# Turned maxima and sums moved from the score ring into packed maximum units, copied by VectorE

## The chip, the cores and the metric

The kernel runs on one core of one Trainium2 chip. The metric is the device time of one execution in microseconds (us), as the median of several runs. A measurement of this kernel tells a change of about 0.2% from none.

## The reference

Two residual blocks run one after the other: differential attention and a gated feed-forward block, each followed by a layer norm.

```
x1  = layernorm(x + attn(x))        # x: 2 batches x 1024 tokens x 128
out = layernorm(x1 + ffn(x1))

# attn: 32 query/key heads of 4 dims, 16 value heads of 8 dims, causal
probs = softmax(q @ k.T * 4 ** -0.5 + causal mask)
attn  = (probs[head, 0] - lam * probs[head, 1]) @ v
attn  = rms_norm(attn) * rms_w * (1 - LAMBDA_INIT), then @ Wo

# ffn: xr, xk mix each token with the one before it
out = sigmoid(xr @ W_r.T) * (relu(xk @ W_k.T) ** 2 @ W_v.T)
```

## The kernel before

**Pairs and bursts.** The 64 (batch, head) score matrices are worked on two at a time, in 32 pairs (`NPAIR`). A pair n has 9 bursts (`NQ`), b = 0 to 8. `pair` of each engine writes the order out by hand: there is one stream of instructions on each engine, and semaphores between them. In burst b TensorE does four things, in this order:

1. `max_unit`: one of the 9 units (`NU`) that compute the scores from which the row maxima come. It runs ahead: in burst b stands unit b + 6 of the next pair for b below 3, and unit b - 3 of pair n + 2 from b = 3 on. The units alternate between two buffers `mx` of two PSUM banks each; unit m waits until VectorE has reduced unit m - 2 (`maxed`).
2. `score_burst`: the two score tiles of burst b (128 keys x 512 queries, one of each matrix), into the ring `ex` of 3 PSUM banks.
3. in burst 6 (`MAXIMA_AT`) `turn_maxima`, in burst 7 (`TURN_AT`) `turn_sums`, both described below.
4. `sum_burst`: the exponentials of four bursts ago times the values, summed in `acc`.

**Engines.** ScalarE takes the exponential of each score tile from `ex` to `e_buf` (L1075); in burst 3 it also copies the sums of the pair before out of `acc` (`take_sums`, L1002), between the two exponentials of that burst, once the sums of burst 3 are made. VectorE reduces each maximum unit to row maxima (L1191 for the plain units, 1024 elements per partition; L1179 for the diagonal ones, 768), combines them after the first unit of burst 3 (`combine`) and splits them in two bf16 parts after the next (`split_low`). GpSimd masks diagonals and normalises. SyncE's queue moves rows.

**Diagonal units.** Two of the nine units hold the diagonal blocks, packed by `diagonal_unit` into 384 of a bank's 512 columns: 8 matmuls of 64 columns (L641), 8 of half the partitions (L650), and 8 that add a mask (L660). They read the array's lower half of rows (partitions 64 to 127), like all maximum units; `score_burst` reads the upper half (0 to 63). Transposes (`turn_...`) use all 128. Before, the diagonal units are units 0 and 1, in bursts 3 and 4.

**What is turned.** `turn_maxima(n + 1)` transposes the combined row maxima (bf16, 128x128) in burst 6; the result is copied to `max_rows` and placed by DMA as rows of `qe`, which pair n + 1's first scores need (`place_maxima`). `turn_sums` transposes the sums of pair n - 1 in burst 7 (two f32 128x128); the result is copied to `o_tok`, from which GpSimd normalises.

**The ring before.** Score tile s of the ring may be written once the exponential of the tile three places before is done (`place_free`). The turned maxima and the turned sums take a place each between the tiles (and one place is skipped), so that a pair has 21 places; their place comes free by a ScalarE copy (`copy_maxima` L947, `store_sums` L1008).

```
def ex_slot(b, i):
    return 2 * b + i + 2 * (b > TURN_AT) + (b > MAXIMA_AT)
```

Of the kernel before, what the change touches and what calls it, by code (L numbers as in the profile page):

```python
# [106 lines left out]
def ex_slot(b, i):  # L107


    return 2 * b + i + 2 * (b > TURN_AT) + (b > MAXIMA_AT)  # L110


SUMS_SLOT = ex_slot(TURN_AT, 1) + 1
MAXIMA_SLOT = ex_slot(MAXIMA_AT, 1) + 1
RING = ex_slot(NQ - 1, 1) + 1
assert RING % EX_BANKS == 0
TILE_AT = {ex_slot(b, i): 2 * b + i for b in range(NQ) for i in range(2)}
# [9 lines left out]
def build(nc, x, Wq, Wk, Wv, Wo, lq1, lk1, lq2, lk2, rms_w, W_r, W_k, W_v, mu_r, mu_k, out):  # L127
# [24 lines left out]
    with ExitStack() as ctx:  # L152
# [84 lines left out]
        last_acc = wide[3][:, 0:HALF]  # L237

# [105 lines left out]
        def _(sp):  # L344
# [268 lines left out]
        def _(pe):  # L613
            def max_unit(g, pr, m):
# [49 lines left out]
            def place_free(n, at):  # L664

                at -= EX_BANKS
                while True:
                    if at < 0:
                        if isinstance(n, int) and n == 0:
                            return  # L670
                        at, n = at + RING, n - 1
                    if at in TILE_AT:
                        wait(pe, s["exped"], 2 * NQ * n + TILE_AT[at] + 1)
                        return
                    if at == SUMS_SLOT and not (isinstance(n, int) and n == 0):
                        wait(pe, s["o_stored"], n)
                        return
                    if at == MAXIMA_SLOT and not (isinstance(n, int) and n == NPAIR - 1):
                        wait(pe, s["max_copied"], n + 2)
                        return  # L680
                    at -= EX_BANKS

            def turn_maxima(n, bank):
# [109 lines left out]
            for u in range(NU + EARLY):  # L793
# [6 lines left out]
                if u == NU + 2:  # L800
                    turn_maxima(0, 2)
# [74 lines left out]
            def pair(g, par, pr):  # L876
# [4 lines left out]
                for b in range(NQ):  # L881
# [37 lines left out]
            turn_sums(NPAIR + 1, 0, last_acc)  # L919
# [18 lines left out]
        def _(act):  # L938
# [3 lines left out]

            def copy_maxima(n, bank):

                wait(act, s["max_rows_in"], 32 * n)
                act.wait_ge(s["max_turned"], n + 1)
                nc.scalar.copy(max_rows[:], ex[:, bank, :].bitcast(BF16)[0:2 * PAIR * NB, 0:P])\  # L947
                    .then_inc(s["max_copied"], 1)
# [47 lines left out]
            copy_maxima(0, 2)  # L996
# [7 lines left out]
            def store_sums(g, par, pr, turned):  # L1004

                act.wait_ge(s["acc_turned"], 2 * g + pr + 1)
                wait(act, s["norm_steps"], NORM_STEPS * (g - 1))
                nc.scalar.copy(o_tok[par][:, 16 * pr:16 * (pr + 1), :],  # L1008
                               turned.rearrange("p (a w) -> p a w", w=VPAD)[:, :, 0:VW + 1])\
                    .then_inc(s["o_stored"], 1)  # L1010
# [50 lines left out]
            def pair(g, par, pr):  # L1061
                static = isinstance(g, int)
                n = 2 * g + pr
                for b in range(NQ):
# [12 lines left out]
                    if b == MAXIMA_AT and not (static and n + 1 >= NPAIR):  # L1077
                        copy_maxima(n + 1, MAXIMA_SLOT % EX_BANKS)
# [341 lines left out]
```

## Time and profile before

| | us |
|---|---|
| median of 3 runs | 438.89 (438.17 to 438.91) |
| the profiled execution, own time | 438.0 |
| its span in the profile | 436.3 |
| TensorE / VectorE / ScalarE / GpSimd busy | 401.9 / 385.8 / 349.2 / 236.5 |

The span is what the trace covers; the execution's own time is 1.7 us longer. Busy time of TensorE is modelled from pipelined matmuls, so a high share does not say that it is at its peak. Three engines are busy over 80% of the span, so the question is which of them waits for which, and where in a pair.

### The profile page before, as it was taken

The numbers are of one execution on the slowest core, as the hardware profiler recorded it, in microseconds if no ns is written. First come the engines' busy times: TensorE is split into PE (matmuls) and PEld (weight loads), VectorE is DVE, ScalarE is ACT, GpSimd is POOL, SyncE is SP. The second block draws the span as 40 slices with busy tenths as digits, with TensorE's granted clock in tenths as the row PEclk, the third lists the DMA queues.
The fourth block names the chain that finished last, engine by engine and source line by source line (L and its number), as shares of the span: only waits on it lengthen the run. The fifth ranks groups of instructions, "written<-read, shape, count | busy, mean of one in ns | idle before, by whom it ended". The sixth has DMA issues, their size and how long they took to land.

```text
span 436.3 us, 17664 instructions
## 1 busy us (share of the span) xinstructions
PE 401.9 (92%) x6209; PEld 197.5 (45%) x6209; DVE 385.8 (88%) x551; ACT 349.2 (80%) x731; POOL 236.5 (54%) x574
## 2 busy tenths in 40 slices
PE   5856999999999999999999999999999999998882
PEld 3522444444444444444444444444444444444462
DVE  1889899999999999999999999999999999893485
ACT  3531799989999999999999999999999999885444
POOL 7200232566666666666666656666666665669422
PEclk9965599999999999999999999999999999998897
DMA  5565264321121111111111111111111121100002
GB/s 142 181 216 159 76 198 147 100 53 51 53 52 49 49 49 49 49 49 49 49 49 49 49 49 49 49 49 49 49 49 49 49 52 27 28 2 2 1 26 73
DMA packets 38800, 28.60 MB, mean 66 GB/s; under 512 B 22368, under 2 KB 27360, under 8 KB 38640
## 3 DMA queue, kind: packets, MB, share of 16 engines
q1 hardware_dynamic: 38176, 27.72, 22.8%
q10 hardware_dynamic: 592, 0.46, 0.4%
q8 instruction: 20, 0.33, 0.3%
q14 instruction: 12, 0.10, 0.1%
HBM read 20.39 MB, written 9.47 MB: 68 GB/s over the span
## 4 chain that ended last, share of the span: by engine, by line
PE 68%; ACT 14%; DVE 6%; issue 5%; DMA 2%; POOL 2%; SPq 1%; ACTq 0%; DVEq 0%; POOLq 0%
PE acc L732 31%; ACT e_buf L1075 13%; PE ex L702 11%; PE mx L629 10%; DVE part_max L1191 3%; PE mx L660 3%; PE ex L740 3%; PE mx L641 2%; PE mx L650 2%; PE ex L686 2%; SPq L335 1%; PE mx L866 1%; DMA x_tok<-in_L_attn_x 1%; PE mx L732 1%; DVE part_max L1179 1%
## 5 line engine op out<-in xcount | busy, mean ns | idle before, releaser
L1075 ACT ACTIVATE e_buf<-ex 128x512 f32<-128x512 f32 x576 | 304.1, 601 | 40.8 <-PE ex L702 40.1
L1191 DVE TENSOR_REDUCE part_max<-mx 128x2 f32<-128x1024 f32 (+2 forms) x224 | 263.9, 1220 | 12.4 <-PE mx L629 9.5
L553 POOL TENSOR_SCALAR_AFFINE_SELECT e_buf<-e_buf 128x256 f32<-128x256 f32 x256 | 100.2, 410 | 157.3 <-ACT e_buf L1075 157.3
L732 PE MATMUL acc<-e_buf,v_grp 128*32 128x256 f32 x2756 | 182.1, 353 | 1.2 <-POOL e_buf L553 1.2
L702 PE MATMUL ex<-qe,ke 26*128 26x512 bf16 (+3 forms) x768 | 148.1, 336 | 0.5 <-ACT e_buf L1075 0.2
L629 PE MATMUL mx<-km,qm 26*128 26x512 bf16 (+2 forms) x768 | 90.8, 301 | 6.2 <-DVE part_max L1191 4.5
L732 PEld LDWEIGHTS acc<-e_buf,v_grp 128*32 128x32 f32 x2756 | 64.9, 109 | 49.4 <-issue 40.7
L1179 DVE TENSOR_REDUCE part_max<-mx 128x12 f32<-128x768 f32 x64 | 61.1, 954 | 7.0 <-PE mx L660 6.1
L629 PEld LDWEIGHTS mx<-km,qm 26*128 26x128 bf16 x768 | 26.8, 93 | 86.5 <-issue 64.0
L702 PEld LDWEIGHTS ex<-qe,ke 26*128 26x128 bf16 x768 | 46.7, 91 | 20.3 <-ACT e_buf L1075 8.6
L536 POOL TENSOR_TENSOR r_rms<-sq_eps,minus_half 128x16 f32<-128x16 f32 x15 | 43.7, 2910 | 0.0
L660 PE MATMUL mx<-mask,pick 32*128 32x192 bf16 (+1 forms) x512 | 26.1, 222 | 0.0
L641 PE MATMUL mx<-km,qm 29*128 29x64 bf16 x512 | 18.9, 193 | 2.9 <-DMA km<-k_rows 2.0
L641 PEld LDWEIGHTS mx<-km,qm 29*128 29x128 bf16 x512 | 11.3, 94 | 21.7 <-issue 11.8
L660 PEld LDWEIGHTS mx<-mask,pick 32*128 32x128 bf16 x512 | 18.4, 95 | 2.8
L650 PE MATMUL mx<-km,qm 29*64 29x64 bf16 x512 | 16.9, 204 | 0.0
L583 POOL TENSOR_TENSOR rs<-ve,minus_half 128x4 f32<-128x4 f32 x8 | 8.5, 1056 | 14.3 <-DVE ve L1268 14.2
L541 POOL TENSOR_TENSOR attn_n<-attn,r_rms 128x32 f32 (+1 forms) x60 | 12.8, 245 | 3.7 <-POOL r_rms L536 3.7
L740 PE MATMUL ex<-identf,o_rows 128*128 128x128 f32 x62 | 13.6, 300 | 0.0
L686 PE MATMUL ex<-identb,turn_max 128*128 128x128 bf16 x32 | 7.4, 231 | 5.6 <-ACT e_buf L1075 4.3
L947 ACT COPY max_rows<-ex 32x128 bf16<-32x128 bf16 x32 | 7.8, 243 | 5.8 <-PE ex L686 5.8
L1002 ACT COPY o_rows<-acc 128x256 f32<-128x256 f32 x31 | 11.6, 373 | 0.9
(144 smaller groups left out, 297.9 us busy)
## 6 DMA issues: line engine op xcount, KB each, us to landing
qm<-q_rows SPq DMA_DIRECT2D x32, 128.0 KB, 2.5
km<-k_rows SPq DMA_DIRECT2D x32, 128.0 KB, 2.7
qe<-q_rows SPq DMA_DIRECT2D x32, 128.0 KB, 2.5
ke<-k_rows SPq DMA_DIRECT2D x32, 128.0 KB, 2.6
q_rows<-part_q SPq DMA_DIRECT2D x6, 256.0 KB, 2.7
k_rows<-part_k SPq DMA_DIRECT2D x6, 256.0 KB, 2.8
q_rows<-part_q SPq DMA_DIRECT2D x6, 192.0 KB
k_rows<-part_k SPq DMA_DIRECT2D x6, 192.0 KB
```

The costliest lines, as they stand in the source:

```text
L536: pool.tensor_tensor(r_rms[:], sq_eps[:], minus_half[:], ALU.pow).then_inc(s["norm_steps"], 1)
L553: pool.affine_select(out=e, in_=e, compare_op=ALU.is_ge, fill=0.0, base=0, pattern=[[0, PAIR], [1, P]], channel_multiplier=-1)\
L629: last = pe.matmul(bank[:, jj, col:col + P * nk], qm[pr][rows, P * qb:P * (qb + 1)], km[pr][rows, P * kb:P * (kb + nk)], start=i == 0, sto ...
L641: pe.matmul(bank[:, jj, BLOCK * r:BLOCK * (r + 1)], qm[pr][rows, t:t + P], km[pr][rows, t:t + BLOCK], start=r == 0, stop=False, skip_group ...
L650: pe.matmul(bank[own, jj, col:col + BLOCK], qm[pr][rows, t:t + BLOCK], km[pr][rows, t:t + BLOCK], start=False, stop=False, skip_group_chec ...
L660: last = pe.matmul(out[:, :, own], pick[rows, c, :], cols, start=False, stop=c == 3, skip_group_check=True)
L702: scored = pe.matmul(ex[:, ex_slot(b, i) % EX_BANKS, col:col + w], ke[pr][rows, P * kb:P * (kb + 1)], qe[pr][rows, q1 - w:q1], start=col = ...
L732: last = pe.matmul(out, v, e, start=first, stop=over, skip_group_check=True)
L740: last = pe.transpose(turned[:, P * i:P * (i + 1)], o_rows[pr][:, P * i:P * (i + 1)], identf[:])
L1075: nc.scalar.activation(e_buf[:, b, i, :], ex[:, ex_slot(b, i) % EX_BANKS, :], ACT.Exp).then_inc(s["exped"], 1)
L1179: nc.vector.tensor_reduce(part_max[pr][:, :, matmuls, 0, :], scores[:, :, 0:BLOCK * ENTRIES] .rearrange("p s (a b) -> p s a b", b=BLOCK), ...
L1191: nc.vector.tensor_reduce(place, scores, AX.X, ALU.max).then_inc(s["maxed"], 1)
```

## The change

The nine maximum units are put in another order: the two diagonal ones become units 3 and 4, so that they stand in bursts 6 and 7 (and three plain units in bursts 3 to 5). The turned maxima are written into the free columns 384 to 511 of unit 3's first bank, the turned sums into those of both banks of unit 4; each transpose is issued at the end of its unit, ahead of the burst's scores, and the unit's semaphore goes up with it. VectorE copies both out, right before it reduces the unit. The ring keeps its 18 score tiles alone. On SyncE's queue `place_maxima` moves ahead of `move_high`, which now waits for unit 4's reduce. For the last pairs, which have no maximum units behind them, the turned data go to other free banks, and VectorE's copies stand between its steps of the first norms.

```diff
 MAX_UNITS = [
-    (0, None),
-    (1, None),
     ([(0, 4, 0, 4)], (slice(1, 2), 1, slice(0, 1))),
     ([(0, 5, 0, 4)], (slice(1, 2), 1, slice(1, 2))),
     ([(0, 6, 0, 4)], (slice(1, 2), 1, slice(2, 3))),
+    (0, None),
+    (1, None),
     ([(0, 7, 0, 4)], (slice(1, 2), 1, slice(3, 4))),
     ([(0, 2, 0, 2), (256, 6, 4, 2)], (slice(0, 2), 2, slice(2, 3))),
     ([(0, 3, 0, 2), (256, 7, 4, 2)], (slice(0, 2), 2, slice(3, 4))),
...
-    return 2 * b + i + 2 * (b > TURN_AT) + (b > MAXIMA_AT)
-
-
-SUMS_SLOT = ex_slot(TURN_AT, 1) + 1
-MAXIMA_SLOT = ex_slot(MAXIMA_AT, 1) + 1
+    return 2 * b + i
+
+
 RING = ex_slot(NQ - 1, 1) + 1
 assert RING % EX_BANKS == 0
-TILE_AT = {ex_slot(b, i): 2 * b + i for b in range(NQ) for i in range(2)}
+
+
+
+MAXIMA_UNIT, SUMS_UNIT = (at + EARLY - NU for at in (MAXIMA_AT, TURN_AT))
+SIDE = BLOCK * ENTRIES
+assert all(isinstance(MAX_UNITS[m][0], int) for m in (MAXIMA_UNIT, SUMS_UNIT)) and MAXIMA_UNIT < SUMS_UNIT
...
+        last_maxima = wide[3].bitcast(BF16)
+        late_sums = wide[2][:, 0:HALF]
+
+        def halves_of(t):
+            return [t[:, P * i:P * (i + 1)] for i in range(2)]
...
-            wait(sp, s["maxed"], NU * n + 2)
+            wait(sp, s["maxed"], NU * n + SUMS_UNIT + 1)
...
+                if not isinstance(n, int) or n + 1 < NPAIR:
+                    place_maxima(sp, n + 1, 1 - pr, g + pr)
                 if not isinstance(n, int) or n + 2 < NPAIR:
                     move_high(sp, n + 2, pr)
-                if not isinstance(n, int) or n + 1 < NPAIR:
-                    place_maxima(sp, n + 1, 1 - pr, g + pr)
...
                     last = diagonal_unit(pr, bank, matmuls)
+                    if m == MAXIMA_UNIT and not (isinstance(n, int) and n < 1):
+                        last = turn_maxima(n - 1, bank[:, 0, :].bitcast(BF16)[:, 2 * SIDE:2 * SIDE + P])
+                    if m == SUMS_UNIT and not (isinstance(n, int) and n < 3):
+                        last = turn_sums(n - 2, 1 - pr, [bank[:, i, SIDE:BANK] for i in range(2)])
...
             def place_free(n, at):
...
+                if isinstance(n, int) and 2 * NQ * n + at < EX_BANKS:
+                    return
+                wait(pe, s["exped"], 2 * NQ * n + at - EX_BANKS + 1)
+
+            def turn_maxima(n, turned):
 
                 pe.wait_ge(s["max_split"], n + 1)
-                pe.transpose(ex[:, bank, :].bitcast(BF16)[:, 0:P],
-                             turn_max[:].rearrange("p e r -> p (e r)"), identb[:]).then_inc(s["max_turned"], 1)
+                return pe.transpose(turned, turn_max[:].rearrange("p e r -> p (e r)"), identb[:])
 
             def score_burst(g, pr, b):
 
...
                     score_burst(g, pr, b)
-                    if b == MAXIMA_AT and not (static and n + 1 >= NPAIR):
-                        place_free(n, MAXIMA_SLOT)
-                        turn_maxima(n + 1, MAXIMA_SLOT % EX_BANKS)
-                    if b == TURN_AT and not (static and n == 0):
-                        place_free(n, SUMS_SLOT)
-                        turn_sums(n, 1 - pr, ex[:, SUMS_SLOT % EX_BANKS, 0:HALF])
+                    if b == MAXIMA_AT and static and n == NPAIR - 2:
+                        pe.wait_ge(s["maxed"], NU * NPAIR)
+                        turn_maxima(NPAIR - 1, last_maxima[:, 0:P]).then_inc(s["max_turned"], 1)
+                    if b == TURN_AT and static and n >= NPAIR - 2:
+                        if n == NPAIR - 1:
+                            pe.wait_ge(s["r_gated"], 1)
+                            pe.wait_ge(s["o_stored"], NPAIR - 2)
+                        turn_sums(n, 1 - pr, halves_of(late_sums)).then_inc(s["acc_turned"], 1)
                     if b == HALF_AT and static and n == NPAIR - 1:
-                        turn_sums(NPAIR, pr, acc[:, 0:HALF])
...
             def take_sums(n, pr):
 
                 act.wait_ge(s["summed"], NQ * (n + 1))
-                wait(act, s["acc_turned"], n - 1)
+                wait(act, s["o_stored"], n - 1)
...
-                    if b == MAXIMA_AT and not (static and n + 1 >= NPAIR):
-                        copy_maxima(n + 1, MAXIMA_SLOT % EX_BANKS)
-                    if b == TURN_AT and not (static and n == 0):
-                        store_sums(g - 1 + pr, par if pr == 1 else 1 - par, 1 - pr,
-                                   ex[:, SUMS_SLOT % EX_BANKS, 0:HALF])
...
-                wait(dve, s["max_turned"], n)
                 nc.vector.tensor_reduce(turn_max[:, 0].rearrange("p (a e) -> p a e", e=4), blocks, AX.X, ALU.max)\
                     .then_inc(s["combined"], 1)
+
+            def copy_maxima(n, turned):
+
+                wait(dve, s["max_rows_in"], 32 * n)
+                nc.vector.tensor_copy(max_rows[:], turned[0:2 * PAIR * NB]).then_inc(s["max_copied"], 1)
+
+            def store_sums(g, par, pr, turned):
+
+                wait(dve, s["norm_steps"], NORM_STEPS * (g - 1))
+                nc.vector.tensor_copy(o_tok[par][:, 16 * pr:16 * (pr + 1), :].rearrange("p (s a) w -> p s a w", s=2),
+                                      turned.rearrange("p s (a w) -> p s a w", w=VPAD)[:, :, :, 0:VW + 1])\
+                    .then_inc(s["o_stored"], 1)
+
+            def take_maxima(n, pr):
+
+                dve.wait_ge(s["max_scored"], NU * (n + 1) + MAXIMA_UNIT + 1)
+                bank = mx_of(n + 1, 1 - pr, MAXIMA_UNIT)
+                copy_maxima(n, bank[:, 0, :].bitcast(BF16)[:, 2 * SIDE:2 * SIDE + P])
+
+            def take_turned(g, par, pr):
+
+                dve.wait_ge(s["max_scored"], NU * (2 * g + pr + 3) + SUMS_UNIT + 1)
+                store_sums(g, par, pr, mx_of(2 * g + pr + 3, 1 - pr, SUMS_UNIT)[:, :, SIDE:BANK])
...
+                    if m - NU == MAXIMA_UNIT:
+                        take_maxima(n + 1, 1 - pr)
+                    if m - NU == SUMS_UNIT and not (static and n == 0):
+                        take_turned(g - 1 + pr, par if pr == 1 else 1 - par, 1 - pr)
...
             norm_attn(0)
+            dve.wait_ge(s["max_turned"], 1)
+            copy_maxima(NPAIR - 1, last_maxima[:, 0:P])
             norm_attn(1)
+            dve.wait_ge(s["acc_turned"], 1)
+            store_sums(NG - 2, 0, 1, late_sums.rearrange("p (s t) -> p s t", s=2))
             apply1(0)
...
             norm_ffn(0)
+            dve.wait_ge(s["acc_turned"], 2)
+            store_sums(NG - 1, 1, 0, late_sums.rearrange("p (s t) -> p s t", s=2))
             normalise_half(0)
```

**TensorE, bursts 6 and 7 of pair 1.** Before (mx is the maximum unit, ex the score tiles, acc the sums):

```order
L629 MATMUL mx<-km,qm 128x512 x2
L702 MATMUL ex<-qe,ke 128x512 x2
L686 MATMUL ex<-identb,turn_max 128x128
L732 MATMUL acc<-e_buf,v_grp 32x128 x8
L629 MATMUL mx<-km,qm 128x512 x2
L702 MATMUL ex<-qe,ke 128x512 x2
L740 MATMUL ex<-identf,o_rows 128x128 x2
L732 MATMUL acc<-e_buf,v_grp 32x256 x4
```

After, up to the transposes of burst 7 (behind them follow the scores and the sums, as in burst 6):

```order
L652 MATMUL mx<-km,qm 128x64 x8
L661 MATMUL mx<-km,qm 64x64 x8
L671 MATMUL mx<-mask,pick 128x6x32 x4
L671 MATMUL mx<-mask,pick 128x2x32 x4
L684 MATMUL mx<-identb,turn_max 128x128
L699 MATMUL ex<-qe,ke 128x512 x2
L729 MATMUL acc<-e_buf,v_grp 32x128 x8
L652 MATMUL mx<-km,qm 128x64 x8
L661 MATMUL mx<-km,qm 64x64 x8
L671 MATMUL mx<-mask,pick 128x6x32 x4
L671 MATMUL mx<-mask,pick 128x2x32 x4
L736 MATMUL mx<-identf,o_rows 128x128 x2
```

The transposes moved from between scores and sums to between the unit and the scores, and the units of these bursts changed from 2 plain matmuls to 24 small ones.

**VectorE, one pair.** Before, from the third unit of a pair (4 + 2 + 1 plain units) to the next pair's two diagonal ones and `split_low`:

```order
L1191 TENSOR_REDUCE part_max<-mx 128x2 x4
L1191 TENSOR_REDUCE part_max<-mx 128x4 x2
L1191 TENSOR_REDUCE part_max<-mx 128x4x2
L1179 TENSOR_REDUCE part_max<-mx 128x2x6
L1198 TENSOR_REDUCE row_max<-part_max 128x16
L1201 TENSOR_REDUCE turn_max<-part_max 128x16
L1179 TENSOR_REDUCE part_max<-mx 128x2x6
L1207 TENSOR_TENSOR turn_max<-row_max,turn_max 128x16
```

After, from the third unit (burst 5) to the ninth, and the next pair's first:

```order
L1165 TENSOR_REDUCE part_max<-mx 128x2
L1180 COPY max_rows<-mx 32x128
L1153 TENSOR_REDUCE part_max<-mx 128x2x6
L1185 COPY o_tok<-mx 128x144
L1153 TENSOR_REDUCE part_max<-mx 128x2x6
L1165 TENSOR_REDUCE part_max<-mx 128x2
L1165 TENSOR_REDUCE part_max<-mx 128x4 x2
L1165 TENSOR_REDUCE part_max<-mx 128x4x2
L1165 TENSOR_REDUCE part_max<-mx 128x2
```

Two copies out of `mx` were added, each ahead of the reduce of a diagonal unit.

**VectorE at the end of the program, behind the last split.** Before, the norms of the first two chunks (`norm_attn(0)`, `norm_attn(1)`) and then `apply1` (L1275):

```order
L1288 TENSOR_TENSOR xT<-mx,x_tok 128x512
L1258 BN_STATS st<-xT 128x6 x4
L1263 BN_AGGR mv<-st 128x2 x4
L1268 TENSOR_SCALAR ve<-mv 128x4
L1288 TENSOR_TENSOR xT<-mx,x_tok 128x512
L1258 BN_STATS st<-xT 128x6 x4
L1263 BN_AGGR mv<-st 128x2 x4
L1268 TENSOR_SCALAR ve<-mv 128x4
L1275 TENSOR_SCALAR x<-xT,mv,rs 128x128 x8
```

After:

```order
L1290 TENSOR_TENSOR xT<-mx,x_tok 128x512
L1260 BN_STATS st<-xT 128x6 x4
L1265 BN_AGGR mv<-st 128x2 x4
L1270 TENSOR_SCALAR ve<-mv 128x4
L1180 COPY max_rows<-mx 32x128
L1290 TENSOR_TENSOR xT<-mx,x_tok 128x512
L1260 BN_STATS st<-xT 128x6 x4
L1265 BN_AGGR mv<-st 128x2 x4
L1270 TENSOR_SCALAR ve<-mv 128x4
L1185 COPY o_tok<-mx 128x144
L1277 TENSOR_SCALAR x<-xT,mv,rs 128x128 x8
```

The copy of the last pair's maxima stands between the two norms, and a copy of turned sums ahead of `apply1`.

## Rows read from the trace of the kernel before

**Rows 1.** Windows: stretch, length; busy us (instructions) by engine; clock, DMA share, GB/s.

```profile
74.58:372.11 297.53, 292.95 (x5052) 138.83 (x5049) 283.36 (x325) 270.51 (x568) 182.89 (x462) 1.00 0.20 50
```

**Rows 2.** Timeline of ScalarE: start, busy us, instructions; maxima copies of pairs 1, 30.

```profile
51.95 0.24 ACT L947 COPY max_rows<-ex 32x128 bf16<-32x128 bf16 x1
...
372.11 0.24 ACT L947 COPY max_rows<-ex 32x128 bf16<-32x128 bf16 x1
```

**Rows 3.** Timeline of TensorE (weight loads apart), one pair, bursts 3 to 8.

```profile
201.51 0.29 PE L641 MATMUL mx<-km,qm 29*128 29x64 bf16 x8
...
201.95 0.39 PE L702 MATMUL ex<-qe,ke 26*128 26x512 bf16 x2
202.02 0.30 PE L660 MATMUL mx<-mask,pick 32*128 32x192 bf16 x6
202.27 0.64 PE L732 MATMUL acc<-e_buf,v_grp 128*32 128x128 f32 x12
202.84 0.29 PE L641 MATMUL mx<-km,qm 29*128 29x64 bf16 x8
...
205.37 0.39 PE L629 MATMUL mx<-km,qm 26*128 26x512 bf16 x2
...
206.02 0.23 PE L686 MATMUL ex<-identb,turn_max 128*128 128x128 bf16 x1 [0.18 <-ACT e_buf L1075]
206.18 0.64 PE L732 MATMUL acc<-e_buf,v_grp 128*32 128x128 f32 x16
206.76 0.39 PE L629 MATMUL mx<-km,qm 26*128 26x512 bf16 x2
...
207.29 0.44 PE L740 MATMUL ex<-identf,o_rows 128*128 128x128 f32 x2
207.65 0.64 PE L732 MATMUL acc<-e_buf,v_grp 128*32 128x256 f32 x8
208.23 0.39 PE L629 MATMUL mx<-km,qm 26*128 26x512 bf16 x2
...
212.58 0.29 PE L641 MATMUL mx<-km,qm 29*128 29x64 bf16 x8
```

**Rows 4.** Timeline of ScalarE, the same pair.

```profile
203.06 0.37 ACT L1002 COPY o_rows<-acc 128x256 f32<-128x256 f32 x1
203.33 3.58 ACT L1075 ACTIVATE e_buf<-ex 128x512 f32<-128x512 f32 x7
206.80 0.24 ACT L947 COPY max_rows<-ex 32x128 bf16<-32x128 bf16 x1
207.22 1.08 ACT L1075 ACTIVATE e_buf<-ex 128x512 f32<-128x512 f32 x2 [0.18 <-PE ex L702]
```

**Rows 5.** Timeline of VectorE, the same pair.

```profile
198.81 3.49 DVE L1191 TENSOR_REDUCE part_max<-mx 128x4 f32<-128x1024 f32 x3
202.46 0.96 DVE L1179 TENSOR_REDUCE part_max<-mx 128x12 f32<-128x768 f32 x1 [0.16 <-PE mx L660]
203.33 0.29 DVE L1198 TENSOR_REDUCE row_max<-part_max 128x16 f32<-128x80 f32 x1
...
203.74 0.95 DVE L1179 TENSOR_REDUCE part_max<-mx 128x12 f32<-128x768 f32 x1
...
204.68 3.73 DVE L1191 TENSOR_REDUCE part_max<-mx 128x2 f32<-128x1024 f32 x3
```

**Rows 6.** The page's part 5: the reduces of plain units.

```profile
L1191 DVE TENSOR_REDUCE part_max<-mx 128x2 f32<-128x1024 f32 (+2 forms) x224 | 263.9, 1220 | 12.4 <-PE mx L629 9.5
```

**Rows 7.** Timeline of VectorE near the end, pair 30.

```profile
383.26 0.68 DVE L1288 TENSOR_TENSOR xT<-mx,x_tok 128x512 f32<-128x512 f32 x1
...
385.37 2.44 DVE L1275 TENSOR_SCALAR x<-xT,mv,rs 128x128 f32<-128x128 f32 x8
```

**Rows 8.** Timeline of TensorE, the same stretch.

```profile
384.57 0.23 PE L686 MATMUL ex<-identb,turn_max 128*128 128x128 bf16 x1
...
386.80 0.66 PE L831 MATMUL mx<-identf,x 128*128 128x128 f32 x4
```

More of the change, by code:

```diff
@@ L377, in _ @@
             load_max_rows(sp, 2, 0)
+            place_maxima(sp, 0, 0, 0)
             move_high(sp, 1, 1)
-            place_maxima(sp, 0, 0, 0)
             fill_rows(1, s["rows_b1"])
@@ L664, in place_free @@
             def place_free(n, at):
[L666 to L683, printed above, removed]
+                if isinstance(n, int) and 2 * NQ * n + at < EX_BANKS:
+                    return
+                wait(pe, s["exped"], 2 * NQ * n + at - EX_BANKS + 1)
+            def turn_maxima(n, turned):
                 pe.wait_ge(s["max_split"], n + 1)
-                pe.transpose(ex[:, bank, :].bitcast(BF16)[:, 0:P],
-                             turn_max[:].rearrange("p e r -> p (e r)"), identb[:]).then_inc(s["max_turned"], 1)
+                return pe.transpose(turned, turn_max[:].rearrange("p e r -> p (e r)"), identb[:])
             def score_burst(g, pr, b):
@@ L739, in turn_sums @@
                 for i in range(2):
-                    last = pe.transpose(turned[:, P * i:P * (i + 1)], o_rows[pr][:, P * i:P * (i + 1)], identf[:])
-                last.then_inc(s["acc_turned"], 1)
+                    last = pe.transpose(turned[i], o_rows[pr][:, P * i:P * (i + 1)], identf[:])
+                return last
             def turn_x(ch):
@@ L799, in _ @@
                     turn_weights()
-                if u == NU + 2:
-                    turn_maxima(0, 2)
             pe.wait_ge(s["wt_scaled"], 1)
@@ L887, in pair @@
                     score_burst(g, pr, b)
-                    if b == MAXIMA_AT and not (static and n + 1 >= NPAIR):
-                        place_free(n, MAXIMA_SLOT)
-                        turn_maxima(n + 1, MAXIMA_SLOT % EX_BANKS)
-                    if b == TURN_AT and not (static and n == 0):
-                        place_free(n, SUMS_SLOT)
-                        turn_sums(n, 1 - pr, ex[:, SUMS_SLOT % EX_BANKS, 0:HALF])
+                    if b == MAXIMA_AT and static and n == NPAIR - 2:
[6 more added lines that the diff above has]
+                        turn_sums(n, 1 - pr, halves_of(late_sums)).then_inc(s["acc_turned"], 1)
                     if b == HALF_AT and static and n == NPAIR - 1:
-                        turn_sums(NPAIR, pr, acc[:, 0:HALF])
+                        turn_sums(NPAIR, pr, halves_of(acc[:, 0:HALF])).then_inc(s["acc_turned"], 1)
                     if b >= LAG:
@@ L918, in _ @@
             sum_burst(NG - 1, 1, 1, NQ - 1)
-            turn_sums(NPAIR + 1, 0, last_acc)
+            turn_sums(NPAIR + 1, 0, halves_of(last_acc)).then_inc(s["acc_turned"], 1)
             turn_attn(2)
@@ L941, in _ @@
             act.dma_start(wv_sb[:], Wv).then_inc(s["wv_in"], 16)
[L943 to L948, printed above, removed]
             def high(m):
@@ L995, in _ @@
             last.then_inc(s["wt_scaled"], 1)
-            copy_maxima(0, 2)
             def take_sums(n, pr):
                 act.wait_ge(s["summed"], NQ * (n + 1))
-                wait(act, s["acc_turned"], n - 1)
+                wait(act, s["o_stored"], n - 1)
                 nc.scalar.copy(o_rows[pr][:], acc[:, 0:HALF]).then_inc(s["acc_copied"], 1)
[L1004 to L1010, printed above, removed]
             def take_half(c):
                 act.wait_ge(s["summed"], NQ * (NPAIR - 1) + (FIRST_HALF if c == 0 else NQ))
-                act.wait_ge(s["acc_turned"], NPAIR - 1)
+                act.wait_ge(s["o_stored"], NPAIR - 2 + c)
                 nc.scalar.copy(o_rows[1 - c][:], acc[:, 0:HALF] if c == 0 else last_acc)\
@@ L1019, in store_half @@
             def store_half(c):
-                act.wait_ge(s["acc_turned"], NPAIR + c)
+                act.wait_ge(s["acc_turned"], 3 + c)
                 act.wait_ge(s["norm_steps"], NORM_STEPS * (NG - 2))
@@ L1219, in _ @@
             for u in range(NU + EARLY):
+                if u == NU + MAXIMA_UNIT:
+                    take_maxima(0, 0)
                 max_unit(0, u // NU, u % NU)
```

## Prediction

> **What bounds the kernel now.** I read the windows first, then the timelines of one steady pair, engine by engine, then the end of the program. Over 297.53 us of steady state TensorE is busy 292.95 us, VectorE 283.36, ScalarE 270.51, all at TensorE's full granted clock (1.00, its 2.4 GHz level) [rows 1]: no engine has much room, and the average does not say who waits. One pair takes (372.11 - 51.95) / 29 = 11.04 us [rows 2].
>
> TensorE's timeline shows two things. First, bursts that the ring holds up: in burst 6 the transpose of the maxima starts 0.65 us after the burst (205.37 to 206.02) and was released by an exponential; in burst 7 the transposes (207.29) stand behind ScalarE's copy of the maxima (206.80 + 0.24). Bursts 6 and 7 take 1.39 and 1.47 us [rows 3, 4]. Second, a burst with a diagonal unit takes 1.33 us (201.51 to 202.84), and in it the scores (201.95) start while the mask matmuls are still going (202.02 to 202.32): unit and scores lie side by side [rows 3].
>
> VectorE is not the bound. Its reduces follow each other at (3.49 - 1.22) / 2 = 1.14 us when nothing holds them [rows 5, 6]; a diagonal one takes 0.87 (202.46 to 203.33), the combining 0.41, the last diagonal reduce and the split 0.94. That is 7 x 1.14 + 0.87 + 0.41 + 0.94 = 10.20 us, so 0.84 of 11.04 is waiting for TensorE [rows 2, 5].
>
> **The change part by part.**
>
> *ScalarE's copies go.* The next work starts 0.42 us after the maxima copy (206.80 to 207.22) [rows 4], of which TensorE's lateness is a part. ScalarE has room already (270.51 of 297.53), so this pays only through the ring.
>
> *The ring.* No score waits for a copy any more. Free of all ring waits, a plain burst is scores to sums 0.32 (201.95 to 202.27), sums 0.58 (207.65 to 208.23): 0.90 us. So burst 6 could gain 1.39 - 0.90 - 0.16 = 0.33 and burst 7 1.47 - 0.90 - 0.37 = 0.20, if nothing else moved (0.16 and 0.37 are the transposes' own shares: 206.02 to 206.18 and 207.29 to 207.65) [rows 3].
>
> *VectorE's two copies.* The trace has no such copy on VectorE. A reduce of 1024 elements takes 1.22 us and one of 768 takes 0.96, so an element is 1.02 ns, and 128 or 144 elements would be 0.31 and 0.32 us alone, 0.23 and 0.24 in a row (0.08 of a reduce's 1.22 overlaps the next). From the other side, ScalarE's same copy takes 0.24 [rows 4 to 6]. I take 0.20 to 0.24 each; the floor of VectorE's pair is then 10.62 to 10.68 us, still below 11.04. They cost nothing while VectorE waits for TensorE ahead of the second diagonal reduce, which the next part makes longer; without that cover they cost 0.44 a pair.
>
> *The diagonal units meet the transposes.* This is the term that decides. The transposes need all array rows, so they wait for the masks, and the scores behind them wait for the transposes: the side by side of unit and scores is gone in both bursts. Masks end at 202.32, 0.81 after the burst's start; the next matmul of other rows starts 0.07 before a modelled end (202.34 against 202.27), so the transpose starts at 0.74. Scores follow 0.16 later (0.90), sums at 1.22, end at 1.22 + 0.57 = 1.79 for burst 6. Burst 7 has 0.37 for 0.16: 2.00 [rows 3]. Together 3.79 us, against 2.86 now. In return bursts 3 and 4 hold plain units, 0.90 each instead of 1.33, where nothing else holds them.
>
> A page speaks against this term. The Trainium skill, TensorE: Matmul & The Clock Gate, in its step-by-step part of what a matmul's phases are for, says that matmuls stay in program order and only weight loads are pulled ahead. The masks stand ahead of the scores in the program, and the trace has scores at 201.95 ahead of six masks at 202.02 [rows 3], so here I go by the rows. By the page there was no overlap to lose, and the two bursts would be 1.33 + 0.16 and 1.33 + 0.37; that is the first rival.
>
> *Does ScalarE give bursts 3 to 5 away?* Count from the start of burst 3. Burst 4 starts at 0.90. The copy of the sums starts 0.22 into it (202.84 to 203.06), 1.12; the next exponential 0.27 later (203.06 to 203.33), 1.39. With burst 3's first exponential at 0.46 (206.76 to 207.22) those of burst 4 start at 1.88 and 2.37 (3.58 us for 7, so 0.49 apart). The second score of burst 5 needs the bank of the one at 1.88: 1.88 + 0.60 + 0.06 = 2.54. Sums at 2.86, burst 6 at 3.43 [rows 3, 4]. So these three bursts cost 3.43, not 2.70: ScalarE's pace, not TensorE's. (0.60 is one exponential's duration by 1.08 for two at 0.49; 0.06 is the hand-over between engines, an estimate from TensorE to ScalarE: 206.76 + 0.39 to 207.22 is 0.07.)
>
> Bursts 8, 0, 1, 2 take 4.35 now (208.23 to 212.58) [rows 3]; I leave them so. TensorE's and ScalarE's loop is then 3.43 + 3.79 + 4.35 = 11.57 us.
>
> *VectorE's loop, counted apart.* From burst 8's start its unit is ready for VectorE at 0.43 (a plain unit takes 0.39, and a hand-over). Then reduces of units 5, 6, 7, 8, 0 (5 x 1.14), combining 0.41, unit 1 in full 1.22 and a hand-over 0.06: 7.82, when TensorE may write unit 3, that is start burst 6. With bursts 6 and 7: 7.82 + 3.79 = 11.61 [rows 3, 5, 6]. The two loops are equal within my reading; I take 11.59.
>
> *The end.* In pair 30 VectorE's `norm_attn(1)` starts at 383.26; now the copy of the maxima stands ahead of it and waits for TensorE's transpose, 384.57 + 0.23. With the copy, the norm starts near 385.04, 1.78 later, and the second copy adds 0.2. `apply1` starts at 385.37, and TensorE takes its result at 386.80 without room to speak of: 1.7 us on the path [rows 7, 8]. Queued behind the waiting copy are both applies and the token mixing, for which TensorE waits.
>
> *Queue of SyncE.* `place_maxima` no longer stands behind `move_high`; the maxima's copy falls 1.3 us into burst 6, before 1.67 (205.37 to 206.80 + 0.24), and the next pair's first scores are later: no wait. `move_high` now starts after burst 7, and its data are needed after the next unit 0, some 5 us on: nothing.
>
> **Sum.** Pairs 0 to 29 have the new bursts: 30 x (11.59 - 11.04) = 16.5, the end 1.7: 438.0 + 18.2 = 456.2 for the profiled execution. The median lies 0.9 above that execution, so 457.
>
> **Rivals.**
> 1. *No overlap to lose* (condition: bursts 6 and 7 at 1.49 and 1.70). TensorE's loop 3.43 + 3.19 + 4.35 = 10.97, VectorE's 7.82 + 3.19 = 11.01: -0.03 x 30 + 1.7, so 439.7 at the median. For it: the starts of matmuls may be modelled. Against: the burst of 1.33 with 24 small matmuls fits only if its scores cost it nothing. Chance 0.07, most of it no change.
> 2. *Only part is lost*: the transposes slip in behind the masks and the scores follow without the gaps of 0.1 at each change. Bursts of 1.6 and 1.8 give a pair of 11.2 to 11.3, and 445 to 449. Chance 0.18.
> 3. *Faster: the freed ring is what counts.* If the transposes hide beside masks and scores altogether, bursts 6 and 7 are 2.66, VectorE's loop 10.48, and the pair falls to VectorE's floor, 10.65: 438.9 - 11.7 + 1.7 = 429. It decides at 3.17 us for both bursts (7.82 + 3.17 + 0.06 of the end = 11.04); above, the kernel is slower. For it are 0.53 us of ring waits in these bursts; against it, the transposes need every row of the array. Chance 0.06.
> 4. *Both loops add up*: each held up by the other in turn, or VectorE's copies uncovered (0.44 a pair): 12.0, 469. Chance 0.07; the two loops pass through different waits, but both end at burst 6's start.
>
> **How the numbers follow.** Forecast (452 to 462) 0.62, rivals as given. A measurement of this kernel tells 0.2%, 0.9 us. Faster: rival 3 and a little of rival 1, 0.08; same: 0.05; slower: 0.87. The range 445 to 463 takes in rival 2 and leaves out the others.
>
> **What would show it.** In the profile after: maxima transposes 11.5 to 11.7 us apart; in bursts 6 and 7 scores starting 0.9 and 1.1 us after the burst's start, and bursts of 1.8 and 2.0; ScalarE idle there for 0.5 us and more each; bursts 3 to 5 held by waits for exponentials; VectorE waiting ahead of the second diagonal unit, the copies 0.2 us each; `norm_attn(1)` 1.8 us later. Scores that start beside the masks, or VectorE without waits, would make the prediction wrong.

## The result, and the profile after

The change makes the kernel slower: 459.92 us (median of 4 runs, 458.17 to 461.11) against 438.53 for the kernel before beside it (4 runs, 438.09 to 438.91), a ratio of 1.0485 (95% interval 1.0443 to 1.0527). The prediction was 457 us in a range of 445 to 463. Disturbed executions are left out of the ratios here and below: one of e7's at 587.69 us, and two of the kernel before beside e9, at 443.97 and 449.48.

The profiled execution took 458.17 us with a span of 456.4, 20.1 more than before. The windows of its trace, with the columns of [rows 1]:

```profile
53.00:59.50 6.50, 6.50 (x86) 2.16 (x82) 3.61 (x4) 4.00 (x8) 1.39 (x4) 0.50 0.13 26
76.96:390.67 313.71, 306.37 (x5056) 141.31 (x5050) 288.73 (x379) 259.07 (x513) 182.28 (x459) 0.99 0.19 49
104.00:114.10 10.10, 9.80 (x173) 4.71 (x165) 9.23 (x13) 8.29 (x17) 6.70 (x21) 1.00 0.21 55
114.10:117.50 3.40, 3.40 (x34) 0.82 (x36) 2.42 (x4) 2.19 (x5) 0.72 (x2) 0.50 0.09 5
```

The second row is the stretch from the 4th to the 31st maxima transpose: 313.71 us for 27 pairs, where 297.53 stood in [rows 1]. One pair takes 11.58 us, the median distance of two of these transposes; before it was 11.02, the mean 297.53 / 27 (the median there is 11.04). The other rows come up under the clock, below.

TensorE's timeline, one steady pair from burst 6 to the next burst 6, and then the last maxima transpose and the first transposes behind the first norm:

```profile
204.72 0.29 PE L652 MATMUL mx<-km,qm 29*128 29x64 bf16 x8 [0.16 <-DVE part_max L1165]
...
205.13 0.40 PE L671 MATMUL mx<-mask,pick 32*128 32x192 bf16 x8
205.46 0.23 PE L684 MATMUL mx<-identb,turn_max 128*128 128x128 bf16 x1
205.62 0.39 PE L699 MATMUL ex<-qe,ke 26*128 26x512 bf16 x2
...
206.51 0.29 PE L652 MATMUL mx<-km,qm 29*128 29x64 bf16 x8
...
207.25 0.44 PE L736 MATMUL mx<-identf,o_rows 128*128 128x128 f32 x2
207.62 0.39 PE L699 MATMUL ex<-qe,ke 26*128 26x512 bf16 x2
...
208.51 0.39 PE L640 MATMUL mx<-km,qm 26*128 26x512 bf16 x2
208.52 0.56 PE L699 MATMUL ex<-qe,ke 26*128 26x384 bf16 x4
...
212.63 0.39 PE L640 MATMUL mx<-km,qm 26*128 26x512 bf16 x2
...
216.30 0.29 PE L652 MATMUL mx<-km,qm 29*128 29x64 bf16 x8
...
404.52 0.23 PE L684 MATMUL mx<-identb,turn_max 128*128 128x128 bf16 x1
...
408.43 0.66 PE L825 MATMUL mx<-identf,x 128*128 128x128 f32 x4 [1.84 <-DVE x L1277]
```

Bursts 6 and 7 last 206.51 - 204.72 = 1.79 and 208.51 - 206.51 = 2.00 us. In both, scores (205.62, 207.62) start only behind the transpose (205.46, 207.25). In [rows 3] they started beside the masks. The scores of burst 8 (208.52) start with their unit (208.51). In the kernel before, whose burst 8 started at 208.23, they did not:

```profile
208.36 0.56 PE L702 MATMUL ex<-qe,ke 26*128 26x384 bf16 x4
```

There the first of them waited for the second exponential of burst 7, which ended at 207.22 + 1.08 = 208.30 [rows 4]: counted in places of the ring, that tile stood three before. In the changed kernel the tile three before is one of burst 6.

VectorE's timeline of the same stretches:

```profile
205.88 0.20 DVE L1180 COPY max_rows<-mx 32x128 bf16<-32x128 bf16 x1
206.01 0.94 DVE L1153 TENSOR_REDUCE part_max<-mx 128x12 f32<-128x768 f32 x1
207.82 0.31 DVE L1185 COPY o_tok<-mx 128x144 f32<-128x144 f32 x1 [0.88 <-PE mx L736]
208.04 0.95 DVE L1153 TENSOR_REDUCE part_max<-mx 128x12 f32<-128x768 f32 x1
208.94 5.75 DVE L1165 TENSOR_REDUCE part_max<-mx 128x2 f32<-128x1024 f32 x5
...
215.02 1.22 DVE L1165 TENSOR_REDUCE part_max<-mx 128x2 f32<-128x1024 f32 x1
...
404.79 0.21 DVE L1180 COPY max_rows<-mx 32x128 bf16<-32x128 bf16 x1 [1.31 <-PE mx L684]
404.93 0.67 DVE L1290 TENSOR_TENSOR xT<-mx,x_tok 128x512 f32<-128x512 f32 x1
...
407.04 0.31 DVE L1185 COPY o_tok<-mx 128x144 f32<-128x144 f32 x1
407.26 0.85 DVE L1277 TENSOR_SCALAR x<-xT,mv,rs 128x128 f32<-128x128 f32 x3
```

The copy of the sums waits 0.88 us for TensorE's transposes (207.82). Behind it runs a stretch in which VectorE waits for nothing: 5 plain reduces (208.94), the combining and one more reduce (215.02), and right behind that TensorE starts burst 6 (216.30); burst 6 of the pair shown waited 0.16 us for such a reduce (204.72). Near the end, the copy of the last maxima waits 1.31 us, and the second norm (404.93) behind it.

ScalarE's timeline of the pair:

```profile
206.04 1.08 ACT L1054 ACTIVATE e_buf<-ex 128x512 f32<-128x512 f32 x2 [1.02 <-PE ex L699]
208.04 5.65 ACT L1054 ACTIVATE e_buf<-ex 128x512 f32<-128x512 f32 x11 [0.92 <-PE ex L699]
```

It waits 1.02 and 0.92 us for the scores of bursts 6 and 7, where [rows 4] had 0.18.

### The profile page after: what moved, and what is told of

Same layout as the page of the kernel before. It is cut to its first block, busy times and chain, and to the rows that moved or that the text cites. A ratio compares the mean times of both kernels' runs of the same rounds, so it can differ in the third digit from the quotient of the medians.

```text
span 456.4 us, 17652 instructions
## 1 busy us (share of the span) xinstructions
PE 417.3 (91%) x6209; PEld 200.9 (44%) x6209; DVE 393.2 (86%) x614; ACT 335.8 (74%) x668; POOL 236.8 (52%) x574
## 4 chain that ended last, share of the span: by engine, by line
PE 45%; DVE 29%; issue 14%; SPq 3%; POOL 2%; DMA 2%; DVEq 1%; ACT 1%; ACTq 1%; POOLq 0%
DVE part_max L1165 20%; PE acc L729 14%; PE ex L699 7%; PE mx L671 5%; PE mx L640 4%; DVE part_max L1153 4%; PE mx L652 3%; PE mx L661 3%; PE mx L736 2%; SPq L342 2%; DVE row_max L1172 1%; PE mx L684 1%; DVE turn_max L1174 1%; PE mx L860 1%; DMA x_tok<-in_L_attn_x 1%
## 5 line engine op out<-in xcount | busy, mean ns | idle before, releaser
L1054 ACT ACTIVATE e_buf<-ex 128x512 f32<-128x512 f32 x576 | 299.9, 601 | 75.3 <-PE ex L699 75.0
L1185 DVE COPY o_tok<-mx 128x144 f32<-128x144 f32 x31 | 9.5, 307 | 25.4 <-PE mx L736 25.4
L736 PE MATMUL mx<-identf,o_rows 128*128 128x128 f32 x64 | 14.0, 300 | 0.5 <-ACT o_rows L995 0.5
L661 PEld LDWEIGHTS mx<-km,qm 29*64 29x64 bf16 x512 | 9.8, 106 | 3.5
```

The costliest lines, as they stand in the source:

```text
L661: pe.matmul(bank[own, jj, col:col + BLOCK], qm[pr][rows, t:t + BLOCK], km[pr][rows, t:t + BLOCK], start=False, stop=False, skip_group_chec ...
L736: last = pe.transpose(turned[i], o_rows[pr][:, P * i:P * (i + 1)], identf[:])
L1054: nc.scalar.activation(e_buf[:, b, i, :], ex[:, ex_slot(b, i) % EX_BANKS, :], ACT.Exp).then_inc(s["exped"], 1)
```

## The experiments

Each ran beside the kernel before, whose median was 437.18 us beside e1 to e4, 438.08 beside e5 to e8 and 437.84 beside e9. "A pair" is the median distance of two maxima transposes; the start is the time up to the 4th of them, the end that behind the 32nd. Pair, start and end come from one profiled execution each; the medians come from 4 to 12 executions.

**e1: the transposes behind the scores.** The change, with each transpose of bursts 6 and 7 issued between scores and sums, as before.

```diff
-                    max_unit(g + 1, pr, m - NU)
+                    max_unit(g + 1, pr, m - NU, later)
                     score_burst(g, pr, b)
+                    if later:
+                        turn_into(n + 2, pr, m - NU).then_inc(s["max_scored"], 1)
```

> The changed kernel with one thing moved: in bursts 6 and 7 of the steady pairs the transposes are issued behind the burst's scores, ahead of the sums; they still go into the free columns of the diagonal units, and VectorE still copies them. Lost overlap (my theory): the scores lie beside the masks again, bursts 6 and 7 fall from 1.79 and 2.00 us to 1.49 and 1.70, the pair from 11.58 to 11.0 (VectorE's loop 7.82 + 3.19), the median from 460 to 442 to 444. Rival, the place in the free columns or VectorE's copies cost the time: 458 to 461, no change. Rival, the order of the units costs it: also no change.

Measured: 445.59 us, ratio 1.0177 (1.0128 to 1.0226); a pair 11.25. TensorE's timeline:

```profile
209.54 0.29 PE L658 MATMUL mx<-km,qm 29*128 29x64 bf16 x8
...
209.98 0.39 PE L705 MATMUL ex<-qe,ke 26*128 26x512 bf16 x2
210.05 0.30 PE L677 MATMUL mx<-mask,pick 32*128 32x192 bf16 x6
210.30 0.23 PE L690 MATMUL mx<-identb,turn_max 128*128 128x128 bf16 x1
...
211.04 0.29 PE L658 MATMUL mx<-km,qm 29*128 29x64 bf16 x8
...
212.73 0.39 PE L646 MATMUL mx<-km,qm 26*128 26x512 bf16 x2
```

Scores (209.98) start beside the masks (210.05) again, and the bursts last 1.50 and 1.69: 0.60 less than 3.79, as expected. The pair gives back only 0.33 of it, so that the time lies above the 442 to 444 that were expected. VectorE's timeline, one pair earlier, says where the rest went:

```profile
201.12 0.31 DVE L1196 COPY o_tok<-mx 128x144 f32<-128x144 f32 x1 [0.62 <-PE mx L742]
...
202.21 5.74 DVE L1176 TENSOR_REDUCE part_max<-mx 128x2 f32<-128x1024 f32 x5
```

Burst 8 started at 201.49, so its unit was ready near 201.92. VectorE still copied sums and reduced the diagonal unit until 202.21: its stretch from there takes 8.05 us instead of 7.79. With shorter bursts the sums' copy, which stands between the transposes and that reduce, is on the path.

**e2: the order alone.** The kernel before with the new order of units and of SyncE's queue. Ring, transposes' places and ScalarE's copies are those of before.

```diff
 MAX_UNITS = [
-    (0, None),
-    (1, None),
     ([(0, 4, 0, 4)], (slice(1, 2), 1, slice(0, 1))),
     ([(0, 5, 0, 4)], (slice(1, 2), 1, slice(1, 2))),
     ([(0, 6, 0, 4)], (slice(1, 2), 1, slice(2, 3))),
+    (0, None),
+    (1, None),
```

> The kernel before with one part of the change alone: the new order of the nine units (diagonal ones in bursts 6 and 7) and the order of SyncE's queue that goes with it; the turned data still take places in the score ring, behind the scores, and ScalarE copies them. Lost overlap: it is kept here, so the pair stays near the one before, 11.0 to 11.3 us, 438 to 447 at the median. Rival, two heavy units ahead of two transposes are too much by themselves, wherever the transposes stand: 11.5 or more, 453 or more.

Measured: 446.4 us, ratio 1.0201 (1.0151 to 1.0251); a pair 11.24. TensorE starts bursts 6, 7 and 8 at 199.95, 201.44 and 203.22, and VectorE's timeline shows waits for the second diagonal unit and for the plain one behind it:

```profile
202.29 0.96 DVE L1179 TENSOR_REDUCE part_max<-mx 128x12 f32<-128x768 f32 x1 [0.17 <-PE mx L660]
203.66 5.92 DVE L1191 TENSOR_REDUCE part_max<-mx 128x2 f32<-128x1024 f32 x5 [0.41 <-PE mx L629]
```

Two heavy bursts side by side (1.49 and 1.78) leave VectorE short, and its stretch of 7.97 us then holds up the next burst 6 (211.19). So the order, with SyncE's queue, costs 0.22 a pair. The stretch is 0.18 longer than the 7.79 of the change. Here the ring still holds up burst 8: its scores start 0.25 behind the unit (203.22),

```profile
203.47 0.56 PE L702 MATMUL ex<-qe,ke 26*128 26x384 bf16 x4
```

the unit of the next burst follows at 204.53, 1.31 later where the change had 1.08, and VectorE, which could have gone on at 203.66 + 1.14 = 204.80, starts its second plain reduce at 204.96. e1 (no ring places, VectorE's copies) and e2 (the ring and the copies of before) have nearly the same pair: what the freed ring gives in that stretch, 0.18, the sums' copy takes again (8.05 in e1).

**e3: a lighter VectorE.** The change, with the reduces of the first two plain units reading half of each stretch of columns. This leaves out a part of the row maxima.

```diff
                     scores = scores[:].rearrange("p s (a b) -> p s a b", a=nh * ne)
+                    if m in (0, 1):
+                        scores = scores[:, :, :, 0:BANK // (2 * nh * ne)]
```

> The changed kernel with VectorE relieved: the reduces of the first two plain units of a pair read half of their columns (the other half of those maxima is left out), 1.07 us less of VectorE a pair. If VectorE's loop alone holds burst 6 back, TensorE starts it when the sums of burst 5 end, 0.2 to 0.3 us earlier: the pair takes 11.3 us, the median 451 to 453. If the loop over ScalarE's pace in bursts 3 to 5 is as long (11.57, as the prediction has it), nothing moves: 458 to 461.

Measured: 454.06 us, ratio 1.0361 (1.0302 to 1.042), a little above the 451 to 453 expected of the case in which VectorE's loop binds alone; pairs alternate between 11.35 and 11.43. The only row of TensorE's steady timeline that still waits is

```profile
211.55 0.64 PE L729 MATMUL acc<-e_buf,v_grp 128*32 128x256 f32 x8 [0.24 <-ACT o_rows L989]
```

That is the other loop, TensorE and ScalarE: 11.39 us, 0.19 under the pair of the change. So the steady pairs of the change are bound by VectorE's loop alone, and the two are not equal.

**e4: ScalarE's copies at the end.** The change, with the turned data of the last pairs copied by ScalarE instead of between VectorE's norms.

```diff
-            dve.wait_ge(s["max_turned"], 1)
-            copy_maxima(NPAIR - 1, last_maxima[:, 0:P])
             norm_attn(1)
```

> The changed kernel with its last part undone: for the last pairs ScalarE copies the turned maxima and sums, at the places where it did before, and VectorE's norms follow each other. If the copies between VectorE's norms cost 1.7 us, the median falls by 1.5 to 2, to 458; if the wait that they cause is hidden further down, no change.

Measured: 456.34 us, ratio 1.0435 (1.0379 to 1.0491), 0.5% under the change, with intervals that overlap. The end takes 48.78 us instead of 51.89. Not all of that is the copies' doing: the end of the change has a stretch of 3.4 us at 1.2 GHz (from 434.95 on), and that of e4 ran at a granted clock of 1.00 from 406.00 to 450.80. The second pair of norms is applied 30.33 us behind the last maxima transpose in the change and 28.82 in e4, so ahead of that stretch the copies cost 1.5 us; the difference grows to 3.1 only behind it.

**e5: the copies doubled.** The change, with each of VectorE's two copies made once more into a spare buffer.

```diff
+                nc.vector.tensor_copy(spare_max[:], turned[0:2 * PAIR * NB])
                 nc.vector.tensor_copy(max_rows[:], turned[0:2 * PAIR * NB]).then_inc(s["max_copied"], 1)
```

> The changed kernel with VectorE's two copies made twice each (the second time into buffers that nobody reads). My prediction held the copies hidden by VectorE's wait ahead of the second diagonal unit. In the trace after, the maxima's copy lies there, but the sums' copy stands behind that wait, and VectorE's next plain reduce starts at 208.94, when its diagonal reduce ends and when its unit is ready alike. If both are hidden: no change, 458 to 461. If the sums' copy is on VectorE's loop: 0.22 us a pair, 11.8 a pair, 464 to 468. If both are: 11.98 a pair, 470 to 473.

Measured: 464.84 us, ratio 1.0592 (1.0543 to 1.0641); a pair 11.75. VectorE's timeline:

```profile
208.68 0.21 DVE L1182 COPY spare_max<-mx 32x128 bf16<-32x128 bf16 x1
208.82 0.20 DVE L1183 COPY max_rows<-mx 32x128 bf16<-32x128 bf16 x1
...
210.68 0.31 DVE L1188 COPY spare_tok<-mx 128x144 f32<-128x144 f32 x1 [0.79 <-PE mx L738]
210.90 0.30 DVE L1190 COPY o_tok<-mx 128x144 f32<-128x144 f32 x1
```

Two more copies, 0.14 and 0.22 from start to start, make the pair 0.17 longer, by most of the second one. The maxima's copy is covered by the wait for the sums' transposes (0.79 where it was 0.88); the sums' copy is not.

**e6: the heavy units apart.** The change, with a plain unit in burst 7 and the second diagonal unit with the turned sums in burst 8.

```diff
     (0, None),
+    ([(0, 7, 0, 4)], (slice(1, 2), 1, slice(3, 4))),
     (1, None),
-    ([(0, 7, 0, 4)], (slice(1, 2), 1, slice(3, 4))),
```

> The changed kernel with the second diagonal unit, and the turned sums with it, moved one burst on, from burst 7 to burst 8, a plain unit between the two heavy ones; the transposes still stand ahead of the scores. If two heavy bursts in a row starve VectorE (it waits 0.88 us ahead of the second), the wait shrinks by 0.4 to 0.8 and the pair goes to about 11.2, 447 to 450. If only the sum of TensorE's work between the loop's ends counts, nothing moves much: 11.5 or more, 456 or more.

Measured: 457.15 us, ratio 1.0418 (1.0372 to 1.0463); a pair 11.52. TensorE starts bursts 6, 7, 8 and 0:

```profile
204.95 0.29 PE L652 MATMUL mx<-km,qm 29*128 29x64 bf16 x8
...
206.75 0.39 PE L640 MATMUL mx<-km,qm 26*128 26x512 bf16 x2
...
207.81 0.29 PE L652 MATMUL mx<-km,qm 29*128 29x64 bf16 x8
...
209.81 0.28 PE L640 MATMUL mx<-km,qm 26*128 26x256 bf16 x2
```

1.80, 1.06 and 2.00 us: the same work, in other places. Spreading alone is worth 0.06 a pair. The theory that VectorE starves behind two heavy bursts in a row does not explain the time of the change: the rival held, as long as the transposes stand ahead of the scores.

**e7: apart, and transposes last.** e6 with e1's place for the transposes; the diffs are theirs.

> The same spread with the transposes behind the scores, as in the first experiment. If starvation and lost overlap are both real and add, this has neither: the pair near 11.0, the median 438 to 441, the same as the kernel before. If spreading brings nothing, 445 as with the transposes moved alone.

Measured: 441.59 us, ratio 1.0073 (1.0046 to 1.01), a little above the 438 to 441 that were expected; a pair 11.02, that of the kernel before. What is left over lies in the start (76.52 us, before 73.67) and the end. TensorE starts bursts 6, 7, 8 and 0, and the scores beside the masks (208.28):

```profile
207.85 0.29 PE L658 MATMUL mx<-km,qm 29*128 29x64 bf16 x8
...
208.28 0.39 PE L705 MATMUL ex<-qe,ke 26*128 26x512 bf16 x2
...
209.34 0.39 PE L646 MATMUL mx<-km,qm 26*128 26x512 bf16 x2
...
210.24 0.29 PE L658 MATMUL mx<-km,qm 29*128 29x64 bf16 x8
...
211.94 0.28 PE L646 MATMUL mx<-km,qm 26*128 26x256 bf16 x2
```

and VectorE has a wait of 0.30 left (0.40 one pair earlier), so its floor is near 10.7:

```profile
211.48 0.31 DVE L1196 COPY o_tok<-mx 128x144 f32<-128x144 f32 x1 [0.30 <-PE mx L742]
```

Moving the transposes is worth 0.50 a pair here and 0.33 in e1.

**e8: e7 with ScalarE's copies at the end** (e4's edit).

> The same, with ScalarE's copies for the last pairs. 1.5 to 3 us less than without: 436 to 439. With the freed ring this is the version that could pass the kernel before; if the ring is worth as little as the trace of the first two experiments says, it does not by more than 1 us.

Measured: 438.18 us, ratio 0.9989 (0.9966 to 1.0012): no change from before that can be told. The end takes 49.50 us, 2.8 less than e7's 52.29. Here too the clock has a part: e7's end has a stretch of 6.8 us at 1.2 GHz (391.9 to 398.7), in which TensorE is busy throughout, and e8's one of 3.4 (from 415.2). The two were not run at like clocks, so the copies' own share of the 2.8 is not shown.

**e9: the first maxima turned early.** e8, with the first pair's maxima turned right behind their split and copied by ScalarE, as before the change.

```diff
                     turn_weights()
+                if u == NU + 2:
+                    turn_maxima(0, ex[:, 2, :].bitcast(BF16)[:, 0:P]).then_inc(s["max_turned"], 1)
```

> Of the profiled execution's 20.1 us over the kernel before, 3.3 fell ahead of the fourth pair, and e7 and e8, whose steady pairs are as fast as before, still lose 2.6 to 2.9 there. Theory: that is the first turned maxima, which wait for a diagonal unit of the next pair (turned at 39.8 instead of 38.1, first scores at 42.9 instead of 41.9 in e8). This kernel is e8 with the first pair's maxima turned by themselves, right behind their split, into a free bank, and copied by ScalarE, as before the change: turned at 38.6, first scores at 41.8, the start 1.0 to 1.4 us shorter than e8's (76.3 to 75.1), the kernel at 436.0 to 437.5, ratio 0.994 to 0.998. Rival: the lost start is the order of the units alone (three plain units ahead of the diagonal ones, so that the combining comes 0.4 to 0.6 us later and TensorE's wait ahead of the first pairs is given by SyncE's and GpSimd's work): no gain over e8, ratio 0.998 to 1.001.

Measured: 438.63 us, ratio 1.0003 (0.9977 to 1.0029): no gain over e8, as the rival had it. The start takes 77.86 us, not less than e8's 76.27. The transpose stands 0.22 us behind the split now (39.81 to 40.03; in e8 38.56 to 39.82), but the split itself was 1.25 later in this execution, and the first scores (43.84) came 3.81 behind the transpose instead of 3.12. In this execution the clock had also fallen to its 1.2 GHz level earlier, at 24.4 instead of 26.1. With 12 and 10 executions at the same median within 0.1%, one transpose is not what the start loses; that it is the order of the units alone, as the rival says, no run shows.

## Why the prediction was right, and where it was not

**The term that decides, "The diagonal units meet the transposes".** Right, to the hundredth: 1.79 and 2.00, together 3.79. e1 and e7 show the cause, the transposes' place: behind the scores the heavy bursts take 1.50 and 1.69 (e7: 1.49 and 1.70), and the pair shortens by 0.33 and 0.50. That it is the rows of the array that the transposes need is how the prediction explained it; the starts fit, but no run put a transpose of half the rows there. The page's rule that matmuls stay in program order (the Trainium skill, TensorE: Matmul & The Clock Gate, Step-by-step: what each phase is for), read as the prediction read it, as no overlap, would have made the place of the transposes in e1 worth nothing. The starts in e1 (scores 209.98, six masks, which stand ahead of them in the program, 210.05) and the bursts 0.60 us shorter do not agree with it. Of the 14 us between the medians of the change and of e1 the pairs make 9.6 in the profiles; 1.1 more is a stretch at the lower clock that only the change has.

**Rivals 1 to 3** are out: the bursts did not come out at 3.19, at 3.4 or at 2.66. Nor is the freed ring with VectorE's copies worth much on balance: 445.59 us in e1 and 446.4 in e2 differ by 0.2%, far inside their intervals. Rival 4's 12.0 is out too, but half of its reason was right, see below.

**"VectorE's loop, counted apart".** 7.82 + 3.79 = 11.61 stands against 7.79 + 3.79 = 11.58 measured, and it is the loop that binds (e3).

**"Does ScalarE give bursts 3 to 5 away?"** The loop of 11.57 was too long by 0.18: e3 measures 11.39. The step at fault is the one that left bursts 8, 0, 1 and 2 "so", at 4.35 us. They take 212.63 - 208.51 = 4.12. The freed ring shortens them (with ScalarE's copies gone), not the order: e2 has the order with ring and copies of before, and there they take 207.63 - 203.22 = 4.41. The prediction looked for the ring's worth in bursts 6 and 7 alone and overlooked that the places of the copies there also hold up burst 8 (its scores 0.13 us behind the unit before, 0.25 in e2, 0.01 in the change). Its reading that burst 7's transposes (207.29) stand behind the copy of the maxima does not fit either: that copy had ended at 207.04. Bursts 3 to 5 take 3.67 with a wait for VectorE of 0.16 in it, so 3.51, where 3.43 was forecast; in e3 the two parts take 4.12 and 3.43 to 3.51. The pair came out right because VectorE's loop was.

**"VectorE's copies cost nothing while VectorE waits".** Half right. They last 0.20 and 0.31 (0.13 and 0.22 from start to start). The maxima's copy is covered. The sums' copy stands behind the wait that should cover it. e5 shows that more work there lengthens the pair, by 0.17 for 0.22: the unit of burst 8 is ready just when the diagonal reduce ends (208.94), so the forecast's count from burst 8, which takes VectorE as free at that moment, is just met, and what is added ahead of it adds to the pair.

**"The end", 1.7 us.** Right where it was priced. Behind the last maxima transpose the second norm starts 0.41 us later instead of 1.31 earlier, so 1.72 later (forecast 1.78), and TensorE's first transposes behind the norms (L825) come after 408.43 - 404.52 = 3.91 us instead of 386.80 - 384.57 = 2.23 [rows 8]: 1.68. At the next norms the change is still 1.5 behind e4. The whole end differs by only 0.2 between the profiles of before and after (51.72 and 51.89), since in before TensorE ran twice at its 1.2 GHz level there (below). In e2, which has the same copies there as the kernel before and no such stretch down to 438, the end takes 50.04. So the small difference of before and after is luck with the clock, and so is a part of the 3.1 and 2.8 us between ends in e4 and e8.

**The start** was priced like any other pair. From the first row to the 4th transpose it is 76.96 us instead of 73.67: 3.3, where three pairs at 0.55 make 1.65.

**The sum.** 27 steady pairs at 0.56 make 15.1, one stretch at the lower clock 1.1, start 3.3, the way from the 31st to the 32nd transpose 0.5 and the end 0.2: 20.2, against 20.1 measured in the profiles and 18.2 forecast. The pair, 16.5 of the 18.2, was right. Left out were the start's other half (1.65) and the stretch at the lower clock (1.1); that the end differed by 0.7 and not by 1.7, because of the clock in the kernel before, took one us off again. So the 2 us between 20.1 and 18.2 are less than what was missed.

## What to carry to other kernels

Do not put a transpose over the whole array between matmuls on one half of its rows and matmuls on the other: here that place alone cost 0.33 and 0.50 us of an 11 us pair. Count each engine's loop from wait to wait, with every unit's ready time, and treat a small copy as free only when it stands ahead of the wait and not behind it. Where two loops come out equal, shorten one on the chip (e3) before believing it. Before comparing a short part of two profiles, such as an end, read the granted clock of both.

## What the hardware did that was not expected

**The clock falls while TensorE is busy.** In the steady state of the changed kernel TensorE's granted clock fell from 1.00 (2.4 GHz) to 0.50 (1.2 GHz) for 3.4 us, after 9.80 busy us of 10.10 (the windows at 104.00 and 114.10 above); the transposes around it lie 12.70 us apart instead of 11.58, so it cost 1.1 us. The profiles of e4 and e5 have two and three such intervals (12.66 to 12.78), those of before, e1 to e3 and e6 to e9 none. The Trainium skill, TensorE: Matmul & The Clock Gate, What's actually happening, describes the lower level as that of an idle TensorE; the trace here disagrees, since ahead of the fall its rows show 0.30 us of idle time in 10.10. What brings it on, no run here settles.

**The start runs longer at the lower clock.** The windows of before:

```profile
53.00:59.50 6.50, 6.37 (x120) 2.70 (x112) 6.27 (x6) 5.66 (x12) 3.15 (x9) 1.00 0.41 139
397.80:401.20 3.40, 3.40 (x24) 1.93 (x22) 1.84 (x5) 1.08 (x2) 3.23 (x3) 0.50 0.00 0
```

From 53.00 on it ran at 1.00; in the changed kernel the same window stands at 0.50, and the clock rose near 59.5. In all ten kernels with a new order of units it rose at 57 to 62 us, and the start is 2.0 (e1, the earliest) to 5.1 us (e6, among the latest) longer than before, in one profiled execution each. What all ten share is that order and that of SyncE's queue. Whether the late rise makes the start long or a longer start delays the rise was not separated. The lower row is one of the two stretches (397.8 to 401.2, 404.6 to 408.0) in the end of the kernel before, which took 51.72 us where e2, without them, took 50.04.
